# One AdaLN transformer block on one core: row sums written to PSUM, the high parts of k and v on ScalarE, three banks for the rest, and other orders

## The reference

```python
h = _layernorm(x) * (1 + ca) + sa
q = (h @ Wq + bq).reshape(b, h, dh, t)      # 16 heads of 8, and so k and v
attn = softmax(einsum('bhdt,bhds->bhts', k, v) * temperature)
x = x + ga * einsum('bhdt,bhts->bhds', q, attn).reshape(b, t, d)
h = _layernorm(x) * (1 + cb) + sb
gate, y = fp4_linear(h, w_gate), fp4_linear(h, w_up)   # 128 -> 352
x = x + gb * fp4_linear(silu(gate) * y, w_down)        # 352 -> 128
```

## Time and profile before

| | us |
|---|---|
| median of 3 runs | 613.52 (611.83 to 613.89) |
| the profiled execution | 614.23 |
| its span, first to last instruction | 611.3 |
| first exponential starts | 24.59 |

### The profile page before, as it was taken

The page is one execution under the profiler, slowest core; times in us unless marked ns, Lnnn a source line. Parts: engine busy times, 40 slices in busy tenths (PEclk is TensorE's granted clock), DMA queues, the critical chain, the costliest instruction groups (busy, mean ns, idle before and its releaser), DMA issues.

```text
span 611.3 us, 15522 instructions
## 1 busy us (share of the span) xinstructions
PE 558.3 (91%) x4336; PEld 385.6 (63%) x4336; DVE 568.7 (93%) x1124; ACT 555.9 (91%) x2281; POOL 507.3 (83%) x710
## 2 busy tenths in 40 slices
PE   4588999999999999999999999999999999998874
PEld 2465556666666666666666666666666666666653
DVE  5568799999999999999999999999999999999986
ACT  2499899999999999999999999999999999999621
POOL 5544478999999999999999999999999999988741
PEclk9669899999999999999999999999999999999878
DMA  5655556546655556555655556655655556652000
GB/s 156 179 142 143 129 152 163 145 133 170 170 140 147 149 155 173 159 157 137 172 144 143 149 155 171 171 145 139 170 144 141 152 153 174 164 143 58 10 10 26
DMA packets 87888, 86.12 MB, mean 141 GB/s; under 512 B 8566, under 2 KB 83548, under 8 KB 87804
## 3 DMA queue, kind: packets, MB, share of 16 engines
q1 hardware_dynamic: 85372, 83.10, 50.4%
q10 hardware_dynamic: 2432, 2.03, 1.2%
HBM read 47.29 MB, written 37.81 MB: 139 GB/s over the span
## 4 chain that ended last, share of the span: by engine, by line
ACT 52%; PE 18%; issue 13%; DVE 12%; POOL 3%; ACTq 1%; DVEq 0%; POOLq 0%
ACT probs L825 47%; DVE neg_max L1005 6%; PE score_ps L1502 6%; PE bank L1581 5%; PE bank L1570 3%; ACT hT L835 2%; DVE silu_g L1123 2%; ACT hid_T L859 2%; PE bank L1548 2%; PE bank L1606 1%; ACT q_T L841 1%; DVE h_mag L975 1%; POOL hid_q L367 1%; PE bank L1520 1%; DVE h_mag L979 1%
## 5 line engine op out<-in xcount | busy, mean ns | idle before, releaser
L825 ACT ACTIVATE probs<-score_ps,neg_max 128x256 f32<-128x256 f32 x1024 | 483.5, 552 | 5.4 <-DVE neg_max L1005 4.3
L1005 DVE TENSOR_REDUCE neg_max<-score_ps 128x4 f32<-128x1024 f32 x256 | 312.1, 1219 | 19.5 <-PE score_ps L1502 16.8
L825 ACT ACTIVATION_READ_ACCUMULATOR probs<-score_ps,neg_max 128x1 f32 x1024 | 292.4, 286 | 0.0
L1502 PE MATMUL score_ps<-v_stack,k_stack 128*128 128x256 f32 x1024 | 234.9, 333 | 24.2 <-ACT probs L825 21.7
L1502 PEld LDWEIGHTS score_ps<-v_stack,k_stack 128*128 128x128 f32 x1024 | 156.0, 194 | 108.2 <-ACT probs L825 85.1
L1548 PE MATMUL bank<-probs,q_z 128*32 128x256 f32 x2048 | 132.6, 389 | 0.0
L1548 PEld LDWEIGHTS bank<-probs,q_z 128*32 128x32 f32 x2048 | 57.6, 111 | 42.4 <-issue 3.2
L1606 PEld LDWEIGHTS bank<-wd_T,hid_T 118*128 118x128 f32 x384 | 52.7, 201 | 7.6 <-ACT hid_T L859 1.3
L1606 PE MATMUL bank<-wd_T,hid_T 118*128 118x128 f32 x384 | 56.0, 286 | 0.5 <-ACT hid_T L859 0.5
L1570 PE MATMUL bank<-wgu_T,h_T 128*128 128x352 f32 x128 | 52.0, 488 | 1.7 <-ACT h_T L848 0.5
L367 POOL TENSOR_TENSOR hid_q<-hid_r,hid_sc 128x704 f32<-128x704 bf16 x31 | 43.0, 1387 | 7.6 <-DVE hid_r L362 7.5
(11 more groups left out here) (119 smaller groups left out, 880.9 us busy)
## 6 DMA issues: line engine op xcount, KB each, us to landing
split_dram<-kv_hi SPq DMA_DIRECT2D x124, 128.0 KB, 2.6
split_dram<-kv_lo SPq DMA_DIRECT2D x124, 128.0 KB, 2.6
...
```

Source lines behind the costliest of these rows:

```text
L825: nc.scalar.activation(probs[p][:, h, a, :], score_ps[:, j % 4, a, :], ACT.Exp, bias=neg_max[:, p, n:n + 1], accum_out=row_sum[:, p, h, a: ...
L1005: nc.vector.tensor_reduce(neg_max[:, p, 4 * u:4 * u + 4], score_ps[:, lo:lo + 2, :, :].rearrange("p b a n -> p (b a) n"), AX.X, ALU.max, n ...
L1502: done = nc.tensor.matmul(score_ps[:, j % 4, a, :], k_stack[p][:, h, 128 * a:128 * a + 128], v_stack[p][:, h // R, :], start=True, stop=True)
```

## The change

Five things are changed together.

1. The row sums of the exponentials go to PSUM. `exps` gives `row_ps`, 64 columns of `bank_3`, as `accum_out` instead of the SBUF tile `row_sum`; a new ACT task `row_sums_out` copies the 32 columns of a batch from there to `row_sum` (for the last batch in four parts).
2. `v_hi` and `k_hi` are ACT tasks now, a Copy and a Copy with a scale. The two low parts stay on DVE, and each waits for both high parts.
3. The bias of q is no matmul any more: `q_out` on ACT adds it as it copies q out of PSUM (Identity with a bias of one value per partition, loaded by a DMA of its own, `b_q`). The constant tiles `b_pad` and `ones_r` get smaller.
4. `bank_3` belongs to the row sums, so that the eight other users of the small banks share three.
5. The lists of all engines have other orders and lags. On POOL, `scale2(b)` waits for DVE's `hid_exponent(b - 2)`, and `shift2(b)` for `hid_magic(b - 2)`.

```diff
-        b_pad = sb("b_pad", [128, 3 * D], F32R)
-        ones_r = sb("ones_r", [128, T], F32R)
+        b_q = sb("b_q", [128, 1])
+        b_pad = sb("b_pad", [128, 2 * D], F32R)
+        ones_r = sb("ones_r", [128, 128], F32R)
...
-        bank_xT, bank_kv, bank_q, bank_h2T, bank_mix, bank_down = bank_1, bank_1, bank_2, bank_0, bank_2, bank_3
-        bank_gate, bank_up, bank_hidT = (bank_2, bank_3), (bank_1, bank_0), (bank_2, bank_0)
-        bank_ffw = (bank_0, bank_3, bank_0)
+        bank_xT, bank_kv, bank_q, bank_h2T, bank_mix, bank_down = bank_0, bank_0, bank_1, bank_1, bank_2, bank_2
+        bank_gate, bank_up, bank_hidT = (bank_0, bank_1), (bank_2, bank_0), (bank_2, bank_1)
+        bank_ffw = (bank_2, bank_1, bank_2)
+
+        row_ps = bank_3[:, 0:2 * H * 2].rearrange("p (b h a) -> p b h a", b=2, a=2)
...
             def scale2(b, c):
+                if 2 <= b < NB - 4:
+                    pool.wait_ge(hid_z_made, b - 1)
                 scale2_on(pool, nc.gpsimd, b, c)
             def shift2(b, c):
+                if 2 <= b < NB - 4:
+                    pool.wait_ge(hid_mag_made, b - 1)
                 shift2_on(pool, nc.gpsimd, b, c)
...
@@ in exps, on ACT
-                                         accum_out=row_sum[:, p, h, a:a + 1]).then_inc(exped, 1)
+                                         accum_out=row_ps[:, p, h, a:a + 1]).then_inc(exped, 1)
+            def row_sums_out(b, c):
+                if b == NB - 1:
+                    return
+                act.wait_ge(exped, 2 * H * (b + 1))
+                wait_batches(act, inv_made, b - 1)
+                nc.scalar.activation(row_sum[:, c % 2, :, :], row_ps[:, c % 2, :, :], ACT.Copy).then_inc(row_sums_made, 1)
...
+            def v_hi(b, c):
+                wait_batches(act, kv_ps_made, b + 1)
+                wait_dma(act, split_stored, b - 2, STORES * 16)
+                nc.scalar.activation(halves(kv_hi[c % 2][:, 1, :]), kv_rows(1), ACT.Copy).then_inc(v_hi_made, 1)
+            def k_hi(b, c):
+                wait_batches(act, kv_ps_made, b + 1)
+                wait_dma(act, split_stored, b - 2, STORES * 16)
+                nc.scalar.activation(halves(kv_hi[c % 2][:, 0, :]), kv_rows(0), ACT.Copy, scale=temp[:, 0:1])\
+                    .then_inc(k_hi_made, 1)
...
@@ in q_out, on ACT
-                nc.scalar.activation(q_T[:, c, :, :], halves(bank_q[:, 0:T]), ACT.Copy).then_inc(qT_made, 1)
+                nc.scalar.activation(q_T[:, c, :, :], halves(bank_q[:, 0:T]), ACT.Identity, bias=b_q[:, 0:1])\
+                    .then_inc(qT_made, 1)
...
@@ in k_lo and in v_lo, on DVE
                 dve.wait_ge(k_hi_made, b + 1)
+                dve.wait_ge(v_hi_made, b + 1)
...
             def row_sums_inv(b, c):
-                wait_batches(dve, exped, b + 1, 2 * H)
+                wait_batches(dve, row_sums_made, b + 1)
...
@@ in q_proj, on PE
-                nc.tensor.matmul(bank_q[:, 0:T], w_q[:, :], hT[:, :], start=True, stop=False)
-                nc.tensor.matmul(bank_q[:, 0:T], b_pad[:, 0:D], ones_r[:, :], start=False, stop=True)\
-                    .then_inc(qT_ps_made, 1)
+                nc.tensor.matmul(bank_q[:, 0:T], w_q[:, :], hT[:, :], start=True, stop=True).then_inc(qT_ps_made, 1)
...
@@ in up_proj, on PE, the half a == 1
-                    wait_bank(b, [(h2T_made, b + 1)], (hidT_made[1], b - 1), (hid_made[1], b))
+                    wait_bank(b, [(silu_made[0], b + 1)], (k_lo_made, b + 5), (v_lo_made, b + 5), (hT_made, b + 5),
+                              (hid_made[1], b))
...
@@ in step(k) of gpsimd
-                if k == 0:
-                    zero_k(0, 0)
...
+                if k == 2:
+                    zero_k(0, 1)
```

607 lines of the change are left out of this document (316 added, 291 removed).

## The result

The changed kernel takes 619.45 us (median of 7 runs, 616.88 to 621.87), the kernel before 611.83 on the same chip (7 runs). The ratio is 1.0124, with a 95% interval of 1.0101 to 1.0147: it is slower by 1.2%. The forecast was 599 us, with a range of 590 to 607. The result lies outside it, and between the times of rival A (607 to 615) and rival B (633). The profiled execution took 621.87 us, the slowest of the seven, with a span of 620.1, which is 8.7 us more than the span before.

The account below looks back on a forecast made before the run. ACT was taken as the bound, fed late once a batch; period 17.18 to 16.6 over 31 intervals gives -18.0, the start +3.1: 614.23 becomes 599.3, less 0.7 for the median 598.6, said as 599 us, range 590 to 607.

Parts of the forecast that it names:

- rival A: Three small banks: last `up_proj` waits for `tanh` and `silu`, PE stands; period near 17.0, 611 us; chance 0.19.
- rival B: ACT's read-out gets no cheaper in PSUM: ACT 17.58, period 17.70, 633 us; slower if period over 17.08; chance 0.17.
- What ACT gets: Work added to ACT per batch: `v_hi` 0.26, `k_hi` 0.355, q's bias 0.095, `row_sums_out` 0.08; sum 0.79 us.
- What ACT may save: 32 read-outs a batch to PSUM at 0.05 instead of 0.09: gain 1.28 us, ACT 17.58 to 16.30.
- feeding: Time per batch in which ACT is fed late: 0.39 us of the 17.18 period, above 16.79 of work.
- with the engines as level as before: Even part: the same 0.24 us as before added to the highest engine, PE at 16.33, for a period of 16.57.
- PE, DVE, POOL: Work per batch: PE 16.63 to 16.33, DVE 16.94 to 16.20, POOL 15.94 to 16.52 with waits.
- POOL's waits: POOL waits 0.6 before `scale2` and 0.25 before `shift2`, 0.85 us a batch, mostly taken up by its idle time.
- the collision: POOL's power beside DVE's `hid_exponent` takes 0.98 against 0.71 elsewhere; the new order removes the 0.27 us.
- The start: Three more memsets and two weight scales on POOL delay the first exponential by 3.1 us, bounds 0 and 5.
- The end: Last two or three slices, a chain of small dependent work: unchanged, plus or minus 2 us.
- The reading of the clock: Profile slices: clock digit is 9 after two slices and stays there; granted clock 1.00, 2.4 GHz, so no clock theory needed.

Follow-up runs that it names:

- Experiments 13 to 15: Changed kernel with DVE's maximum over two heads made as one per head, for heads 6 to 7, 6 to 9, 6 to 11: 622.25, 620.46, 612.81 us.
- Experiment 4: Changed kernel without POOL's two new waits, before `scale2` and `shift2`: 620.72 us, ratio 1.0108 to the kernel before.

## Why the prediction was wrong

**What ACT gets** was right: 0.79 forecast, by last writes 0.267 + 0.364 + 0.086 + 0.087 = 0.80.

**What ACT may save** is the step that failed: "I take 0.05 for a read-out into PSUM, a gain of 32 x 0.04 = 1.28." The step of 0.05 is there, but a start is not the price. By last writes the gain is 0.029, which makes 0.93, and four other instructions give back 0.029 each. Net 0.81. The base had the same fault: 16.79 of work and 0.39 of feeding were 17.03 and 0.15. The forecast of 16.30 stood against 17.02 measured. Put rightly, the sum would have said: no change on ACT. Rival B gave its point of decision in two forms, a gain under 25 ns and an ACT over 16.78. By the first (29 ns) it had not come, by the second (17.02) it had, because the base under it was too low as well.

The period was to fall by 0.58 and rose by 0.16. Of this 0.74, 0.47 is the saving. The rest is feeding, which was to go from 0.39 to 0.3 over ACT's work and went from 0.15 to 0.33.

**Feeding.** I added what was lost before, "with the engines as level as before". That put the period 0.27 above ACT's 16.30. By last writes the loss was 0.15 before, and it became 0.33. Experiments 13 to 15 show most of this: the work of a pair of heads on ACT fell from 1.82, just under, to 1.70, well under the 1.84 that scores and a maximum over two heads need between two pairs that share banks. A saving on exponentials that follow each other could not be cashed there. Rows of before could have told it: the maximum of 1.2, two heads' exponentials of 1.8, and the scores.

**PE, DVE, POOL.** PE's busy time fell to 16.41 a batch (47.31 of 50 us), for 16.33 forecast. DVE's fell to 16.50 (47.58), for 16.20: only 0.44 of the 0.74 came off, and no run shows why. POOL's fell to 15.40 (44.40). Experiment 4 shows POOL's waits to cost nothing in this kernel. The power of the second half takes 0.71, as against 0.98; with the waits taken out, `scale2` takes 1.00 for 0.73. So the collision is avoided, but it was not on the path.

**The start** was right in size, 3.27 for 3.1, and partly by luck. POOL's power did move from 4.72 to 8.06 behind the memsets and scales. But VectorE's first variance, which the sum did not look at, moved as well, because its order has two passes over the weights ahead of it. It ends at 7.81, where it ended at 4.49, so POOL alone could have given back only 0.25 (an estimate from these rows, the first of the kernel before):

```profile
4.33 0.16 DVE L1013 TENSOR_REDUCE var<-stats 128x2 f32<-128x4 f32 x1
```
```profile
7.65 0.16 DVE L1058 TENSOR_REDUCE var<-stats 128x2 f32<-128x4 f32 x1
```

**The end** was within the 2 allowed: the exponentials of the last batch took 1.17 less and what follows them 1.18 more. The reading of the clock had a slip that changes nothing: its digits are below 9 in the second, third and fifth slice too.

**Rival A** did not happen: PE is not idle before the last `up_proj`, and 0.1 before the `gate_proj` ahead of it. What it said of the chain was partly right, in that `silu` lies in the chain before head 6, but on DVE's side and not through the small bank.

The prediction named its own test, "I am wrong altogether if the read-out is cheap and the period still stays at 17", and it was met: the step of the read-out is 0.05 and the period 17.34.
